# Routing of two mixtures of experts by fewer, wider operations, and identity products nobody reads on TensorE in its waits

## The reference

```python
x = x + tanh(g_xattn[0]) * L0_xattn(ln(x), ctx, mask)   # stage 0: 16 heads of 8
x = x + tanh(g_ffn[0])   * L0_ffn(ln(x))                # stage 1: mixture, 16 experts, top 4
x = x + tanh(g_xattn[1]) * L1_xattn(ln(x), ctx, ctx)    # stage 2
x = x + tanh(g_ffn[1])   * L1_ffn(ln(x))                # stage 3: 128 -> 512 -> 128
x = x + tanh(g_xattn[2]) * L2_xattn(ctx, ln(x))         # stage 4: 8 heads of 64
x = x + tanh(g_ffn[2])   * L2_ffn(ln(x))                # stage 5: 8 experts, top 2
x = x + tanh(g_xattn[3]) * L3_xattn(ln(x), ctx, ctx)    # stage 6: 16 heads of 8
x = x + tanh(g_ffn[3])   * L3_ffn(ln(x))                # stage 7: mixture, 64 experts, top 6
```

```python
# stage 1: E=16, G=4 groups, TG=2, K=4
scores = sigmoid(x @ router.T); sc = scores + bias
group  = sum(top_2(sc in each group)); keep the 2 best groups, others' sc -> 0
idx    = top_4(sc); w = scores[idx] / (sum + 1e-20) * 2.5
# stage 7: E=64, G=8 groups, TG=4, K=6
scores = sigmoid(x @ gate.T) + bias
group  = max(scores in each group); keep the 4 best groups, others -> 0
w, idx = top_6(scores); w = w / (sum + 1e-8)
# both: y = sum_e w_e * down_e(silu(gate_e x) * up_e x) + shared expert
```

## Time and profile before

| | us |
|---|---|
| median of 3 runs | 643.35 |
| lowest and highest | 641.51 and 653.01 |
| profiled execution | 643.2 |
| its span, first to last instruction | 641.1 |
| mean granted TensorE clock over the span | 0.954 |
| TensorE busy | 589.4 (92%) |
| VectorE busy | 392.3 (61%) |
| ScalarE busy | 375.5 (59%) |
| GpSimd busy | 221.4 (35%) |

### The profile page before, as it was taken

The page is one execution under the profiler, slowest core; times in us unless marked ns, Lnnn a source line. Parts: engine busy times, 40 slices in busy tenths (PEclk is TensorE's granted clock), DMA queues, the critical chain, the costliest instruction groups (busy, mean ns, idle before and its releaser), DMA issues.

```text
span 641.1 us, 10297 instructions
## 1 busy us (share of the span) xinstructions
PE 589.4 (92%) x3526; PEld 400.0 (62%) x3526; DVE 392.3 (61%) x739; ACT 375.5 (59%) x752; POOL 221.4 (35%) x209
## 2 busy tenths in 40 slices
PE   8999986999998998999897998899985899999997
PEld 6466754786664445776553444467753688888885
DVE  4578839464633346777145665388849566666665
ACT  4377774556644336888543444477773456666663
POOL 5007664581000000000000434000023288888884
PEclk9999988999988998999898999899987799999999
DMA  8200001340000000000000101000001256655550
GB/s 281 87 2 2 2 1 42 92 98 21 2 1 1 0 0 1 1 3 1 2 0 0 37 13 61 1 2 3 1 6 37 63 165 180 180 175 173 174 150 34
DMA packets 14850, 33.53 MB, mean 52 GB/s; under 512 B 2912, under 2 KB 8432, under 8 KB 14672
## 3 DMA queue, kind: packets, MB, share of 16 engines
q1 hardware_dynamic: 14800, 32.89, 17.3%
HBM read 32.03 MB, written 0.85 MB: 51 GB/s over the span
## 4 chain that ended last, share of the span: by engine, by line
PE 76%; DVE 8%; issue 8%; ACT 7%; POOL 2%; ACTq 0%; DVEq 0%; POOLq 0%
PE bank L726 8%; PE bank L727 8%; PE bank L728 8%; PE bank L643 5%; PE bank L654 4%; PE bank L669 3%; PE bank L957 3%; PE bank L617 3%; PE bank L608 3%; PE bank L572 2%; ACT wa L1266 2%; PE bank L1101 2%; PE bank L967 2%; PE bank L1126 2%; PE bank L1124 2%
## 5 line engine op out<-in xcount | busy, mean ns | idle before, releaser
L726 PE MATMUL bank<-xn_hi,w_hi 128*128 128x512 f32 x168 | 69.1, 411 | 14.1 <-DVE wc L1728 7.1
L453 POOL TENSOR_TENSOR h_lo<-wc,h_hi 128x512 fp32r<-128x512 f32 x56 | 72.4, 1296 | 19.8 <-ACT h_hi L1335 19.8
L728 PE MATMUL bank<-xn_hi,w_lo 128*128 128x512 f32 x168 | 68.4, 407 | 0.0
L727 PE MATMUL bank<-xn_lo,w_hi 128*128 128x512 f32 x168 | 68.3, 407 | 0.0
L1752 DVE TENSOR_TENSOR wb<-arena,bank 128x512 f32<-128x512 f32 x64 | 44.0, 687 | 33.3 <-PE bank L728 33.2
L1335 ACT ACTIVATE h_hi<-wc 128x512 fp32r<-128x512 f32 x56 | 35.4, 633 | 44.4 <-DVE wc L1760 29.8
L1547 DVE TENSOR_TENSOR wa<-bank,row_max 128x512 f32<-128x512 f32 x64 | 44.2, 691 | 7.5 <-ACT wb L1212 4.3
L1543 DVE TENSOR_REDUCE row_max<-bank 128x4 f32<-128x512 f32 x64 | 43.6, 681 | 8.1 <-PE bank L643 7.5
L1212 ACT ACTIVATE wb<-wa 128x512 f32<-128x512 f32 x64 | 40.1, 630 | 13.8 <-DVE wa L1547 13.4
L445 POOL TENSOR_TENSOR w_lo<-ring,w_hi 128x384 fp32r<-128x384 f32 x42 | 42.8, 1020 | 15.5 <-ACT w_hi L1312 15.5
L534 POOL TENSOR_TENSOR x<-x,upd 128x128 f32 x8 | 6.0, 753 | 120.6 <-ACT upd L1202 120.6
(11 more groups left out here) (286 smaller groups left out, 1307.8 us busy)
## 6 DMA issues: line engine op xcount, KB each, us to landing
arena<-comb_rows SPq DMA_DIRECT2D x64, 256.0 KB, 4.0
ring<-in_experts SPq DMA_DIRECT2D x42, 192.0 KB, 2.4
ring<-in_experts SPq DMA_DIRECT2D x8, 256.0 KB, 3.5
mats<-in_mats SPq DMA_DIRECT2D x1, 1472.0 KB, 9.7
mats<-in_mats SPq DMA_DIRECT2D x1, 832.0 KB, 5.5
mats<-in_mats SPq DMA_DIRECT2D x2, 320.0 KB, 7.8
x<-in_x_t SPq DMA_DIRECT2D x1, 512.0 KB, 4.1
context<-in_ctx_t SPq DMA_DIRECT2D x1, 512.0 KB, 4.8
```

What stands on the lines that cost most here:

```text
L453: nc.gpsimd.tensor_tensor(h_lo[:, v % 3, :], hidden_of(v), h_hi[:, v % 3, :].bitcast(f32), ALU.subtract).then_inc(m_h_lo, 1)
L726: mm(out, w, x_, start=start, stop=False)
L727: mm(out, w, x_rest, start=False, stop=False)
L728: return mm(out, w_rest, x_, start=False, stop=stop)
```

## The change

Routing, on VectorE:

- `route_groups` of the second mixture: `ranks` is replaced by a memset, MAX8 and MATCH_REPLACE8 for each of the 8 tiles on the 8 groups' scores and four very large constants (12 elements), and one comparison. The first mixture keeps `ranks`.
- `route_top`: the 8 multiplies become one over all tiles; the comparison at its end goes.
- `route_weights`: the comparison is now part of the first multiply (`scalar_tensor_tensor`); for the first mixture the factor 2.5 goes into the sum (times 0.4 before the reciprocal) and its own operation goes.
- Tiles move: the picked weights lie at 512 instead of 1568, and `turn_full` reads them there.

On TensorE `keep_warm(n, to)` runs n products of the identity with itself (128 x 128, plain 32-bit) into a bank that is free there; nobody reads them and nothing is signalled. They stand: behind the means of the norms of stages 1, 6 and 7 (2, 3, 2); behind the norm of stage 6 (4); in each attention's wait for the second half of the q rows (5, behind a wait for the first of them, so that bank 4 is free); in the last batch's tail (2, 3, 2, 2); and in the mixtures behind `gate_up(1)` and `gate_up(3)` (4 each in the first, 9 each in the second). The wait for `a_vtok` moves from behind the norm of stage 6 to before it.

```diff
--- before.py
+++ after.py
@@ -554,6 +554,10 @@
                 for _ in range(n):
                     mm(to[:, 0:P], idle_w, idle_w, start=True, stop=True)
 
+            def keep_warm(n, to):
+                for _ in range(n):
+                    mm(to[:, 0:P], ident[:, :], ident[:, :], start=True, stop=True)
+
             def norm_stats(i, c):
 
                 src, dst, affine, (kind, s) = NORMS[i]
@@ -591,8 +595,9 @@
                 for c in range(2):
                     norm_spread(i, c)
 
-            def norm(i):
+            def norm(i, idle=0):
                 norm_means(i)
+                keep_warm(idle, bank[4])
                 norm_rest(i)
 
             def bias_spread():
@@ -690,6 +695,8 @@
                 scores(0, 0)
                 scores(0, 1)
                 q_rows_of(inst, 1)
+                pe.wait_ge(a_q_rows, 8 * inst + 5)
+                keep_warm(5, bank[4])
                 pe.wait_ge(a_q_rows, 8 * inst + 8)
                 for b in range(B):
                     for u in range(4):
@@ -703,8 +710,13 @@
                         if b > 0:
                             tail(b - 1, u)
                 probs_v(B - 1, 3)
-                for u in range(4):
-                    tail(B - 1, u)
+                keep_warm(2, bank[3])
+                tail(B - 1, 1)
+                keep_warm(3, bank[3])
+                tail(B - 1, 2)
+                keep_warm(2, bank[3])
+                tail(B - 1, 3)
+                keep_warm(2, bank[3])
 
             def bias_through_o(inst):
 
@@ -763,7 +775,7 @@
                     pe.wait_ge(m_pick, n + 1)
                     for j in range(BH):
                         last = nc.tensor.transpose(bank[6 + c][0:m["E"], j * P:j * P + P],
-                                                   routing(1568, 2 * BH, m["E"])[:, BH * c + j, :], ident[:, :])
+                                                   routing(512, 2 * BH, m["E"])[:, BH * c + j, :], ident[:, :])
                     last.then_inc(m_full, 1)
 
                 def combine_t(c):
@@ -774,7 +786,13 @@
                                                    comb_pieces[:, BH * c + j, :], ident[:, :])
                     last.then_inc(m_combT, 1)
 
-                for v in range(6):
+                for v in range(2):
+                    gate_up(v)
+                keep_warm(4 + 5 * n, bank[5])
+                for v in range(2, 4):
+                    gate_up(v)
+                keep_warm(4 + 5 * n, bank[5])
+                for v in range(4, 6):
                     gate_up(v)
                 for c in range(2):
                     turn_full(c)
@@ -838,7 +856,7 @@
             pe.wait_ge(a_vtok, 2)
             pe.wait_ge(ln_out, 2)
             attn(0)
-            norm(NORM_OF[1][0])
+            norm(NORM_OF[1][0], 2)
             moe(MOE[0])
 
             w = mats1
@@ -1141,14 +1159,15 @@
             bias_through_o(1)
             attn_v(1, 0, bank[4])
             attn_v(1, 1, bank[5])
-            norm(i6)
             pe.wait_ge(a_vtok, 4)
+            norm(i6, 3)
+            keep_warm(4, bank[5])
             pe.wait_ge(tgb_ready, 4)
             pe.wait_ge(ln_out, 2 * i6 + 1)
             q_rows_of(1, 0)
             pe.wait_ge(ln_out, 2 * i6 + 2)
             attn(1)
-            norm(NORM_OF[7][0])
+            norm(NORM_OF[7][0], 2)
             moe(MOE[1])
 
 
@@ -1669,10 +1688,22 @@
                     link(v.tensor_tensor(t3, lo[:, :, :, 0], lo[:, :, :, 1], ALU.max))
                     link(v.tensor_tensor(t2, t2, t3, ALU.max))
                     link(v.tensor_tensor(best, t1, t2, ALU.add))
+                    rank = ranks(best, G, m["tri"], 0)
+                    link(v.tensor_scalar(routing(2240, TILES, G), rank, float(m["TG"]) - 0.5, None, ALU.is_lt))
                 else:
-                    link(v.tensor_reduce(best, biased.rearrange("p t (g s) -> p t g s", g=G), X, ALU.max))
-                rank = ranks(best, G, m["tri"], 0)
-                link(v.tensor_scalar(routing(2240, TILES, G), rank, float(m["TG"]) - 0.5, None, ALU.is_lt))
+
+                    width = G + 8 - m["TG"]
+                    ext, cut = routing(2400, TILES, width), routing(2400 + TILES * width, TILES, width)
+                    v.memset(ext[:, :, G:width], 3e38)
+                    link(v.tensor_reduce(ext[:, :, 0:G], biased.rearrange("p t (g s) -> p t g s", g=G), X, ALU.max))
+                    top = routing(2304, TILES, 8)
+                    for t in range(TILES):
+                        ins = v.max(top[:, t, :], ext[:, t, :])
+                    link(ins)
+                    for t in range(TILES):
+                        ins = v.match_replace(cut[:, t, :], top[:, t, :], ext[:, t, :], -3e38)
+                    link(ins)
+                    link(v.tensor_scalar(routing(2240, TILES, G), cut[:, :, 0:G], -1e38, None, ALU.is_lt))
 
             def route_top(m):
 
@@ -1684,11 +1715,8 @@
                 width = E + 8 - K
                 ext, cut = routing(1024, TILES, width), routing(1568, TILES, width)
                 v.memset(ext[:, :, E:width], 3e38)
-                for t in range(TILES):
-                    ins = v.tensor_tensor(ext[:, t, 0:E].rearrange("p (g s) -> p g s", g=G),
-                                          groups[:, t, :, :],
-                                          keep[:, t, :].unsqueeze(2).to_broadcast([P, G, size]), ALU.mult)
-                link(ins)
+                link(v.tensor_tensor(ext[:, :, 0:E].rearrange("p t (g s) -> p t g s", g=G), groups,
+                                     keep.unsqueeze(3).to_broadcast([P, TILES, G, size]), ALU.mult))
                 top = routing(2304, TILES, 8)
                 for t in range(TILES):
                     ins = v.max(top[:, t, :], ext[:, t, :])
@@ -1696,26 +1724,25 @@
                 for t in range(TILES):
                     ins = v.match_replace(cut[:, t, :], top[:, t, :], ext[:, t, :], -3e38)
                 link(ins)
-                link(v.tensor_scalar(routing(512, TILES, E), cut[:, :, 0:E], -1e38, None, ALU.is_lt))
 
             def route_weights(m):
 
                 n, E, K = m["n"], m["E"], m["K"]
                 ext = routing(1024, TILES, E + 8 - K)
-                chosen = routing(512, TILES, E)
+                cut = routing(1568, TILES, E + 8 - K)[:, :, 0:E]
                 weight = routing(0, TILES, E) if n == 0 else ext[:, :, 0:E]
-                picked = routing(1568, TILES, E)
-                link(v.tensor_tensor(picked, weight, chosen, ALU.mult))
+                picked = routing(512, TILES, E)
+                link(v.scalar_tensor_tensor(picked, cut, -1e38, weight, ALU.is_lt, ALU.mult))
                 total = arena[:, 16384 + 2368:16384 + 2368 + TILES]
                 link(v.tensor_reduce(total, picked, X, ALU.add))
-                link(v.tensor_scalar(total, total, 1e-20 if n == 0 else 1e-8, None, ALU.add))
+                if n == 0:
+
+                    link(v.tensor_scalar(total, total, 1e-20, 0.4, ALU.add, ALU.mult))
+                else:
+                    link(v.tensor_scalar(total, total, 1e-8, None, ALU.add))
                 link(v.reciprocal(total, total))
                 share = total.unsqueeze(2).to_broadcast([P, TILES, E])
-                if n == 0:
-                    link(v.tensor_tensor(picked, picked, share, ALU.mult))
-                    v.tensor_scalar(picked, picked, 2.5, None, ALU.mult).then_inc(m_pick, 1)
-                else:
-                    v.tensor_tensor(picked, picked, share, ALU.mult).then_inc(m_pick, 1)
+                v.tensor_tensor(picked, picked, share, ALU.mult).then_inc(m_pick, 1)
                 dve.wait_ge(m_pick, n + 1)
                 split_weights(picked, E).then_inc(m_comb, 2)
```

## The result

The changed kernel took 622.14 us (median of four executions, 620.22 to 626.22), the kernel before 643.38 beside it: a ratio of 0.9685, 95% interval 0.9661 to 0.9709. The forecast was 628.5 with 624 to 636 as its range. The profiled execution took 621.75 us.

The account below looks back on a forecast made before the run. The prediction took TensorE to bound the kernel, delayed by VectorE's routing in both mixtures and by low clock. Gains of 5.4, 8.0, 0.3 and 1.0 us made 14.7, so 643.2 became 628.5 us, range 624 to 636.

Parts of the forecast that it names:

- the sum: Whole kernel: gains of 5.4, 8.0, 0.3 and 1.0 make 14.7 us, so 643.2 becomes 628.5.
- The chance of 0.07: Whole kernel: a gain over 18 us, because a fall avoided in a norm shifts what follows; chance 0.07.
- rival 1: Mixtures: the clock still falls in the 12-product groups, giving 633.8 with three falls, 639.5 at worst; chance 0.17.
- Mixture 0, 5.4: First mixture: one wide product, shorter routing and full-clock products bring L765 5.4 us earlier.
- Mixture 1, 8.0: Second mixture: MAX8 ranking, one wide product and full-clock products bring L765 8.0 us earlier.
- its bound: Second mixture's `route_groups`: MAX8 and MATCH_REPLACE8 on 12 elements take at most the 2.10 us of 20 elements.
- Outside the mixtures: Identity products in attentions and norms of stages 1 and 7: 0.3 us gained; norm of stage 6: 1.0 net.
- norm 6: Norm of stage 6: L617 at full clock gains 1.5 us, the earlier copy wait loses 0.5; net 1.0 gained.
- 2 (MAX8 blocked by GpSimd): Routing in both mixtures: MAX8 is held up by GpSimd, 6.3 us come back, 634.8 us; chance 0.10.
- The rule that the prediction weighed there: Routing on VectorE: instructions with at most one SBUF input, outside two-port modes, don't contend with GpSimd; otherwise 634.8 us.
- 3 (slower, products that don't hold the clock): All places with identity products: they run at the low level ahead of real work, 4.1 us lost, 647.3; chance 0.04.
- 4 (lost race): `route_top`, both mixtures: the wide product starts after GpSimd, 2.6 us lost, 631; within the forecast's own range.

Follow-up runs that it names:

- e7_more: The changed kernel with further identity products in norms 3, 4 and 5, both heads in stages 2 to 5 and elsewhere; 620.21 us, ratio 0.961 at first.
- e10_before_low_spots: The kernel before with only those further identity products of e7_more that lie in stages 2 to 5; 637.66 us.
- after_again: The changed kernel, unchanged, traced in another execution; 628.79 us.
- e1: The changed kernel without any identity product and with the wait for `a_vtok` 4 where it was before; 631.4 us.
- e4: The changed kernel without the identity products within the two mixtures; 623.7 us.
- e5: The changed kernel with identity products only in norms 1, 6 and 7, none in attentions or mixtures; 630.28 us (622.83 to 635.37).
- e2: The changed kernel with all its identity products but the routing of the kernel before; its time lies within 636 to 642 us.
- e8: e7_more with the routing of the kernel before; 13.6 us slower than e7_more.
- e9: e7_more without the identity products behind `gate_up(1)` and `gate_up(3)` in the mixtures; median 1.4 us from that of e7_more, within 621.5 to 624 us.

## Why the prediction was wrong

**The step that failed** is in the sum: it adds the touched places and takes everything else of the profiled execution as it was ("643.2 - 14.7 = 628.5"), stages 2 to 5 among it. None of its rows shows them, though they held five of the thirteen low stretches ahead of the end, which are worth 7.1 us between all low and none (e7_more, e10_before_low_spots), half of the forecast gain. In the first trace of the changed kernel 6.4 us of them were gone, in after_again nothing. The chance of 0.07 "for a gain over 18 us, since a fall avoided in a norm shifts what follows" names the right mechanism. It was far too small (five of eleven executions have such a gain), and the range's lower end of 624 gave it no room. The clue stood in the times of before, 641.5 to 653.0 in three executions; the prediction used it for rival 1 alone, as a loss.

**The terms**, by its own steps:
- Mixture 0, 5.4: 5.3 to 5.4. The wide product won its race and took 0.26 us (0.3 forecast); `gate_up(4)` to L777 took 2.84 (2.75). L777 came at 110.47, 4.5 us earlier in a trace whose start was 0.8 later.
- Mixture 1, 8.0: 8.6. MAX8 on 12 elements took less than its bound. On the other side L1676, the bias addition, took 1.78 us beside GpSimd, and 1.40 before.
- Their reason was half wrong. The sum gave the full clock to the identity products. With the short routing the clock stayed full with them in all six traces and fell without them in four of five, but such a fall costs 0.7 us at most (e1, e4, e5); with the old routing e2 and e8 lack it in spite of them, behind a wait of 3.52 us in e8. The two terms were right in size, and the shorter wait for VectorE is the cause of nearly all of them.
- Outside the mixtures: 0.5 for drains and norms instead of 0.3, 1.2 instead of 1.0 for norm 6, in all three traces. This is the worth in executions whose partner in before had a low clock there for one stretch; e4 against e1 shows 7.7 us between medians of four executions each.
- Start-up: not in the sum, and 1.2 to 1.7 us lost in the three traces. The diff does nothing there; four of the five other traces of before have the same (1.5 to 1.8), so it was the first trace of before that was lucky.

**The rivals.** 1 (the clock still falls in the mixtures): no, 1.00 from 98 to 112 and 466 to 486 us in the first trace, and none in the two others. 2 (MAX8 blocked by GpSimd): no, 0.75 us for eight, with L453 running. The rule that the prediction weighed there (the Trainium skill, SBUF — State Buffer, Who interferes with whom) agrees with that row. 3 (slower, products that don't hold the clock): no. 4 (lost race): no. The forecast of 628.5 is the time of one kind of execution, and the measured median that of the other; over eleven executions the median, 626.0, would lie within the range given. That after_again met 628.5 within 0.3 us is partly luck: 1.7 us lost at start-up stand against small gains elsewhere that were not forecast either.

## What to carry to other kernels

When the profile shows a clock that is low in places which the change doesn't touch, read each of them and put its worth into the range: shifting the work can make any of them go or come, and one profile is one draw. Compare kernels over some ten executions, or take the variation out first by covering the thin spots. Here that gave the best version, e7_more, at 620.7 us (median of ten, 620.0 to 621.6), against 626.0 of the changed kernel (median of eleven) and medians of 642 to 647 of before. Four identity products in front of a wait of 3.5 us did not hold the clock; shorten the wait first. With the short routing the clock held with them, which was worth 0.7 us at most. Before trusting a median that did not move, look into the trace: the clock had fallen in e4 and the time did not tell.

## What the hardware showed that I had not expected

- The clock fell behind a wait of 0.97 us and small products (L576, 128x1) in after_again and not in the first trace, stayed full behind waits of 2.46 and 1.81 us in e9, and fell behind one of 2.46 us in e4. The length of the wait alone doesn't tell.
- The instants at which falls begin keep their distance (187.73 us in three traces) while a step between lies 184.2 to 184.6 us behind the first of them.
- In e1 the clock stayed low for 13.3 us over a fully busy TensorE (the head of attention 1: 101 instructions where 177 ran at full clock). Its products there are small, 128x128 and 32x128; that this is why is not shown.
- MAX8 on 12, 20 and 66 elements took 0.68, 0.75 and 1.13 us for eight, beside GpSimd or not.
